# Six transformer layers with 16-head window attention: Wv times Wo formed per head on chip, values wide, no output projection

## The reference

```python
def shift_tokens(t):                       # second half of the channels comes from the token before
    a, s = jnp.split(t, 2, -1)
    s = jnp.pad(s, ((0, 0), (1, 0), (0, 0)))[:, :-1]
    return jnp.concatenate([a, s], -1)

def attn_layer(x, Wqkv, qs, ksc, Wo):      # 16 heads of 64: Wqkv 128 x 3072, Wo 1024 x 128
    q, k, v = sh(x @ Wqkv)
    q, k = l2norm(q) * qs, l2norm(k) * ksc
    q, k = rotary(q) * scale, rotary(k) / scale
    out = local_attention(q, k, v)         # window of 32 queries looks at its own 32 keys and the 32 before
    return out.transpose(0, 2, 1, 3).reshape(b, n, INNER) @ Wo
...
for i in range(DEPTH):                     # 6
    x = attn_layer(shift_tokens(x), Wqkv[i], q_scale[i], k_scale[i], Wo[i]) + x
    x = ffn_layer(shift_tokens(x), ln_g[i], ln_b[i], W1[i], b1[i], W2[i], b2[i]) + x
```

## Time and profile before

| | |
|---|---|
| median of 3 runs | 3265.14 us (3257.32 to 3265.72) |
| profiled execution, its own time | 3262.19 us |
| its span, first to last instruction | 3260.4 us |
| PE busy | 3129.7 us, 96% |
| ACT, DVE, POOL busy | 2717.7 (83%), 2687.9 (82%), 2560.2 (79%) |
| DMA, mean traffic | 69 GB/s; the one hardware queue takes 25.8% of the 16 engines' time |
| mean granted TensorE clock | 0.995 of full |

### The profile page before, as it was taken

How to read it: one execution, slowest core, us unless ns; L and a number is a source line. 1 busy time by engine, 2 the same in 40 slices (tenths; PEclk the granted TensorE clock), 3 DMA queues, 4 the chain that set the end, 5 groups by cost and what they waited for, 6 DMA issues and landing times.

```text
span 3260.4 us, 154019 instructions
## 1 busy us (share of the span) xinstructions
PE 3129.7 (96%) x65394; PEld 2384.6 (73%) x66148; DVE 2687.9 (82%) x4034; ACT 2717.7 (83%) x4817; POOL 2560.2 (79%) x2557
## 2 busy tenths in 40 slices
PE   8998799999999999999999999999999999999998
PEld 6886577777777777777777777777777777677776
DVE  6887888888888888888888888888888888788884
ACT  5665688888888888888888888888888888888886
POOL 3433988888888888888888888887888888788882
PEclk9999999999999999999999999999999999999999
DMA  1000332232233223223322322322332332332231
GB/s 47 29 2 28 83 79 73 75 78 68 71 75 86 69 71 80 70 64 88 82 61 74 79 67 77 85 70 63 78 78 72 78 75 67 86 75 62 65 76 52
DMA packets 140219, 224.69 MB, mean 69 GB/s; under 512 B 29456, under 2 KB 41360, under 8 KB 139152
## 3 DMA queue, kind: packets, MB, share of 16 engines
q1 hardware_dynamic: 139536, 214.78, 25.8%
HBM read 21.72 MB, written 4.19 MB: 8 GB/s over the span
## 4 chain that ended last, share of the span: by engine, by line
PE 93%; issue 3%; DVE 1%; POOL 1%; ACT 1%; DMA 0%; SPq 0%; POOLq 0%; DVEq 0%; ACTq 0%
PE bank L1021 12%; PE bank L954 11%; PE bank L906 11%; PE bank L1037 10%; PE bank L980 9%; PE bank L1367 8%; PE bank L907 7%; PE bank L999 5%; PE bank L1380 4%; PE bank L905 3%; PE bank L364 2%; PE bank L344 2%; PE bank L329 2%; PE bank L1352 1%; PE bank L1342 1%
## 5 line engine op out<-in xcount | busy, mean ns | idle before, releaser
L1284 POOL TENSOR_TENSOR rotbuf<-mbuf 128x512 f32<-128x512 f32 x768 | 975.1, 1275 | 340.4 <-PE bank L954 326.2
L1173 DVE TENSOR_TENSOR mbuf<-bank,table 128x512 f32<-128x512 f32 x768 | 522.5, 680 | 341.2 <-ACT sq L1063 290.0
L1298 POOL TENSOR_TENSOR rotbuf<-rotbuf,rs 128x512 f32<-128x512 f32 x768 | 788.9, 1043 | 14.9
L1063 ACT ACTIVATE sq<-bank 128x512 f32<-128x512 f32 x768 | 458.8, 597 | 154.7 <-PE bank L907 140.4
L1174 DVE TENSOR_TENSOR mbuf<-bank,table 128x512 f32<-128x512 f32 x768 | 522.8, 681 | 0.0
L906 PE MATMUL bank<-weights,inputs 128*128 128x512 bf16 x1152 | 438.4, 381 | 70.3 <-issue 45.3
L1021 PEld LDWEIGHTS bank<-probs_t,vbuf 64*64 64x64 f32 x24576 | 394.5, 134 | 115.7 <-issue 115.1
L954 PE MATMUL bank<-ident,rotbuf 128*128 128x128 f32 x3072 | 449.3, 279 | 17.6 <-POOL rotbuf L1298 7.8
L1155 DVE TENSOR_REDUCE ss<-sq 128x16 f32<-128x1024 f32 x384 | 459.4, 1196 | 0.0
L907 PE MATMUL bank<-weights,inputs 128*128 128x512 bf16 x1152 | 438.2, 380 | 0.0
L1021 PE MATMUL bank<-probs_t,vbuf 64*64 64x32 f32 x24576 | 437.3, 220 | 0.1
(11 more groups left out here) (119 smaller groups left out, 5736.5 us busy)
## 6 DMA issues: line engine op xcount, KB each, us to landing
vbuf<-v_stage SPq DMA_DIRECT2D x1152, 128.0 KB, 2.4
vbuf<-v_stage SPq DMA_DIRECT2D x576, 64.0 KB, 2.1
stage<-in_wqkv SPq DMA_DIRECT2D x36, 256.0 KB, 3.0
weights<-in_wo SPq DMA_DIRECT2D x6, 512.0 KB, 3.9
out_t<-weights SPq DMA_DIRECT2D x1, 2048.0 KB, 6.3
weights<-out_t SPq DMA_DIRECT2D x1, 2048.0 KB, 11.5
out_t<-weights SPq DMA_DIRECT2D x16, 128.0 KB, 2.0
wffn<-in_w SPq DMA_DIRECT2D x6, 341.0 KB, 3.1
```

The source lines that it names most:

```text
L1173: e.tensor_tensor(b.m1[:, u % 2, :].rearrange("p (h s d) -> p h s d", h=8, s=2), pj, cos, ALU.mult)
L1284: e.tensor_tensor(b.rot[:, u, :], b.m1[:, u % 2, :], b.m2[:, u % 2, :], ALU.add).then_inc(s.rotated, 1)
L1298: e.tensor_tensor(v, v, r, ALU.mult).then_inc(s.scaled, 1)
```

## The change

Out = sum over heads of P_h (x Wv_h) Wo_h is computed as sum over heads of P_h (x (Wv_h Wo_h)). Wv_h Wo_h is 128 x 128 for each head, formed once a layer on chip and split into bf16 hi and lo; the values of a token have 16 x 128 = 2048 columns (1024 before) in 8 parts; `pe_values_of` takes transposed probabilities as the stationary operand (4 heads x 32 keys on 128 partitions, 32 queries) and values as the moving one (128 columns), so that heads, key halves and head groups add up in one bank, tokens on partitions; two transposes (`pe_transpose_out`) take the place of `pe_project_out`. Keys, scores, masks and probabilities are kept in halves by even and odd window of 32. The freed bank becomes a fourth work bank. The weights carry Wv (transposed, with zeros for the other head of a pair) and Wo side by side in `wvo`; q and k columns come as `wqk`. Wo is no longer loaded on its own. All lists and the ring have a new order.

Core of the diff:

```diff
-PLACED = (160, 128)
+VALUE_COLS = HEADS * DIM
+VALUES = 2 * VALUE_COLS // 512
+PLACED = (256, 256)
...
+WORK_BANKS = 4
+FIRST_BANKS = 3
 WORK_RING = (
+    ("t", 3, 1), ("t", 4, 1), ("v", 0, 2), ("wv", 0, 1), ("out", 0, -1), ("pj", 3, 2), ("pj", 4, 2),
+    ("t", 5, 1), ("pj", 5, 2), ("v", 1, 2), ("up", 0, -2), ("up", 1, -2), ("t", 6, 1), ("pj", 6, 2),
+    ("v", 2, 2), ("pj", 7, 2), ("up", 2, -2), ("t", 7, 1), ("pj", 0, 3), ("v", 3, 2), ("v", 4, 2),
+    ("pj", 1, 3), ("mu", 0, -1), ("v", 5, 2), ("t", 0, 2), ("dn", 0, -2), ("t", 1, 2), ("pj", 2, 3),
+    ("v", 6, 2), ("v", 7, 2), ("t", 2, 2),
 )
...
-STAGE = 512
-STAGE_PIECES = 3 * INNER // STAGE
-STAGE_FROM, SPLIT_FROM, OUTER_AT = 2, 3, 4
-LATE_AT = {9: 0, 11: 1, 13: 2}
+STAGE, STAGE_FUSED = 512, 768
+SPLIT_PIECES, FUSED_PIECES = 2 * INNER // STAGE, VALUE_COLS // 512
+STAGE_PIECES = SPLIT_PIECES + FUSED_PIECES
+STAGE_FROM, SPLIT_FROM, FUSE_FROM, OUTER_AT = 3, 2, 5, 4
+LATE_AT = {11: 0, 13: 1}
...
+def fused_piece(k):
+    piece = k.seq - FUSE_FROM
+    return piece if k.ok and k.layer + 1 < DEPTH and 0 <= piece < FUSED_PIECES else None
...
-    col = 2 * INNER + 512 * half
+    col = 2 * INNER + 512 * part
...
-            e.wait_ge(s.att_ready, k.layer + 1)
...
+    staged = b.stage[:, (SPLIT_PIECES + i) % 2, :].rearrange("p (c r d) -> p c r d", c=2, r=3)
+    for group in range(4):
+        parity, chunk = divmod(group, 2)
+        mm = e.matmul(bank[:, DIM * group:DIM * (group + 1)], staged[:, chunk, parity, :], staged[:, chunk, 2, :], start=True, stop=True)
+    return mm
...
+def pe_fuse(e, s, b, at, ahead):
+    k = at(ahead)
+    i = fused_piece(k)
+    if i is None:
+        return
+    pe_wait_bank(e, s, at, "wv", 0)
+    e.wait_ge(s.staged[(SPLIT_PIECES + i) % 2], 16 * staged_count(k.layer + 1, SPLIT_PIECES + i))
+    fuse_products(e, b, work_bank(b, k, "wv", 0), i).then_inc(s.fused, 1)
...
+        return
+    e.wait_ge(s.fused, FUSED_PIECES * (k.layer + 1) + i + 1)
+    if i == 0 and k.layer > 0:
+        e.wait_ge(s.v_full, VALUES * (FIRST_N + k.layer * SEQS))
+    e.activation(b.wh[(k.layer + 1) % 2][:, fused_columns(i)], work_bank(b, k, "wv", 0)[:, :], ACT.Copy).then_inc(s.fused_hi, 1)
...
+    e.wait_ge(s.fused_hi, FUSED_PIECES * (k.layer + 1) + i + 1)
+    hi, lo = (w[(k.layer + 1) % 2][:, fused_columns(i)] for w in (b.wh, b.wl))
+    e.tensor_tensor(lo, work_bank(b, k, "wv", 0)[:, :], hi, ALU.subtract).then_inc(s.fused_lo, 1)
...
+    base = KEY_SLOT * (SLOTS * par + slot)
+    if window % 2:
+        first, step = base + 16 * (window - 1), KEY_ODD
+    else:
+        first, step = base + 16 * window, KEY_ODD - (WINDOW if window else 0)
+    return b.kflat[r, first:first + 2 * step].rearrange("p (a k) -> p a k", a=2)[:, :, 0:WINDOW]
-                              b.q[r, slot, first:first + WINDOW], b.k[r, k.par, slot, first:first + SPAN_K],
+                              b.q[r, slot, first:first + WINDOW], window_keys(b, r, k.par, slot, 4 * t + quarter),
...
-        e.wait_ge(s.out_copied, k.c[STEPS] + t)
-    for j in range(2):
-        for quarter in range(4):
-            for odd, parity in ((0, 0), (1, 1), (0, 1), (1, 0)):
-                r, out_r = slice(64 * odd, 64 * odd + 64), slice(64 * parity, 64 * parity + 64)
-                value = DIM_HEAD * (4 * half + 2 * j + parity)
-                prob = P * (2 * parity + j) + WINDOW * quarter
-                out = P * (2 * half + j) + WINDOW * quarter
-                mm = e.matmul(b.outs[odd][out_r, out:out + WINDOW], b.v[r, k.par, 4 * t + quarter, value:value + DIM_HEAD],
-                              b.deep_ptf[r, i % 2, prob:prob + WINDOW], start=True, stop=True)
+    terms = [(pair, odd, quarter) for pair in range(2) for odd in range(2) for quarter in range(4)
+             if 4 * t + quarter - (quarter % 2 != odd) >= 0]
+    for pair, odd, quarter in terms:
+        group = 2 * half + pair
+        block = 4 * t + quarter - (quarter % 2 != odd)
+        rows = slice(WINDOW * quarter, WINDOW * (quarter + 1))
+        prob = P * (2 * pair + odd) + WINDOW * quarter
+        mine = [x for x in terms if x[2] == quarter]
+        mm = e.matmul(b.out_nat[rows, DIM * t:DIM * (t + 1)], b.deep_ptf[:, i % 2, prob:prob + WINDOW],
+                      b.v[:, k.par, block, DIM * group:DIM * (group + 1)],
+                      start=half == 0 and (pair, odd, quarter) == mine[0], stop=half == 1 and (pair, odd, quarter) == mine[-1])
...
-def pe_project_out(e, s, b, at, ahead):
+def pe_transpose_out(e, s, b, at, ahead):
-    e.wait_ge(s.out_copied, k.c[STEPS] + STEPS)
-    out = work_bank(b, k, "out", 0)[:, 0:N_TOK]
-    for chunk in range(INNER // P):
-        mm = e.matmul(out, b.wo[k.layer % 2][:, chunk, :], b.ot8[:, chunk, :], start=chunk == 0, stop=chunk == INNER // P - 1)
-    mm.then_inc(s.proj_full, 1)
+    e.wait_ge(s.out_copied, k.c[1] + 1)
+    out = work_bank(b, k, "out", 0)
+    for t in range(2):
+        mm = e.transpose(out[:, P * t:P * (t + 1)], b.on[:, DIM * t:DIM * (t + 1)], b.ident[:, :])
+    mm.then_inc(s.out_full, 1)
...
-    t, half = divmod(i, 2)
-    e.wait_ge(s.v_full, k.c[4] + (i + 1))
-    if half == 0:
+    t, part = divmod(i, 4)
+    e.wait_ge(s.v_full, k.c[VALUES] + (i + 1))
+    if part == 0:
         e.wait_ge(s.v_placed[t], k.c[PLACED[t]])
...
+    if not k.ok:
+        return
+    e.wait_ge(s.pv_full, k.c[SUBS] + SUBS)
+    e.wait_ge(s.out_full, k.c[1])
+    e.activation(b.on, b.out_nat, ACT.Copy).then_inc(s.out_copied, 1)
...
-    e.tensor_tensor(b.probs[:, t, :, :].rearrange("p (b h) k -> p b h k", b=2), b.deep_scores,
-                    b.deep_max[:, t, :].rearrange("p (b h) -> p b h", b=2).unsqueeze(3).broadcast_to([P, 2, SLOTS, SPAN_K]),
-                    ALU.subtract).then_inc(s.shifted, 1)
+    e.tensor_tensor(b.probs[:, t, :, :, :].rearrange("p o h k -> p h o k"), b.scores_by_half,
+                    b.deep_max[:, t, :].unsqueeze(2).unsqueeze(3).broadcast_to([P, HEADS, 2, WINDOW]), ALU.subtract).then_inc(s.shifted, 1)
...
-    for odd in range(2):
-        r, col = 64 * odd, slice(512 * odd, 512 * (odd + 1))
-        e.wait_ge(s.v_copied, k.c[4] + (odd + 1))
-        e.dma_start(b.v[r + 32:r + 64, k.par, 0, :], b.vstage[0:32, 0, col]).then_inc(s.v_placed[0], 16)
-        e.dma_start(b.v[r:r + 64, k.par, 1, :], b.vstage[0:64, 0, col]).then_inc(s.v_placed[0], 16)
...
-        e.dma_start(b.v[r:r + 64, k.par, 7, :], b.vstage[64:128, 1, col]).then_inc(s.v_placed[1], 16)
+    for t in range(2):
+        for part in range(4):
+            e.wait_ge(s.v_copied, k.c[VALUES] + (4 * t + part + 1))
+            for block in range(4):
+                e.dma_start(b.v[WINDOW * part:WINDOW * (part + 1), k.par, 4 * t + block, :],
+                            b.vstage[WINDOW * block:WINDOW * (block + 1), t, 512 * part:512 * (part + 1)]).then_inc(s.v_placed[t], 16)
...
+def sp_stage_weights(e, s, b, layer, i):
+    taken = layer * STAGE_PIECES + i - 2
+    if taken >= 0:
+        of, piece = divmod(taken, STAGE_PIECES)
+        if piece < SPLIT_PIECES:
+            e.wait_ge(s.split, SPLIT_PIECES * of + piece + 1)
+        else:
+            e.wait_ge(s.fused, FUSED_PIECES * of + piece - SPLIT_PIECES + 1)
+    if i < SPLIT_PIECES:
+        e.dma_start(b.stage[:, i % 2, 0:STAGE], b.wqk[layer, :, STAGE * i:STAGE * (i + 1)]).then_inc(s.staged[i % 2], 16)
+    else:
+        e.dma_start(b.stage[:, i % 2, :], b.wvo[layer, :, i - SPLIT_PIECES, :]).then_inc(s.staged[i % 2], 16)
...
-        piece, rest = divmod(k.seq - STAGE_FROM, 2)
-        if rest == 0 and 0 <= piece < STAGE_PIECES:
-            sp_stage_attention(e, s, b, k.layer + 1, piece)
+        piece = k.seq - STAGE_FROM
+        if 0 <= piece < STAGE_PIECES:
+            sp_stage_weights(e, s, b, k.layer + 1, piece)
-    piece, rest = divmod(k.seq - SPLIT_FROM, 2)
-    if k.ok and k.layer + 1 < DEPTH and rest == 0 and 0 <= piece < STAGE_PIECES:
-        pool_split_attention(e, s, b, k.layer + 1, piece)
+    piece = k.seq - SPLIT_FROM
+    if k.ok and k.layer + 1 < DEPTH and 0 <= piece < SPLIT_PIECES:
+        pool_split_weights(e, s, b, k.layer + 1, piece)
```

More of the change, by code:

```diff
@@ L204, in first_bank @@
 def first_bank(b, kind, i):
-    return b.work[first_place(kind, i) % WORK_BANKS]
+    return b.work[first_place(kind, i) % FIRST_BANKS]
 def pe_first_wait_bank(e, s, at, kind, i):
     j, size = first_place(kind, i), len(FIRST_RING)
-    for back in range(WORK_BANKS, 6 * size, WORK_BANKS):
+    for back in range(FIRST_BANKS, 6 * size, FIRST_BANKS):
         slots = 0 if j >= back else 1 + (back - j - 1) // size
@@ L750, in __init__ @@
         self.x_ready, self.first_done = first.normed[1], FIRST_N + SEQS
-        self.att_staged = [sem(f"att_staged{i}") for i in range(2)]
-        self.att_hi = sem("att_hi")
-        self.att_split = sem("att_split")
+        self.staged = [sem(f"staged{i}") for i in range(2)]
+        self.split_hi = sem("split_hi")
+        self.split = sem("split")
+        self.fused = sem("fused")
```

(58 more changed lines are left out.)

309 lines of the change are left out of this document (158 added, 151 removed), and 4 rows, old and new, of the table WORK_RING.

## The result

The changed kernel takes 3772.95 us (median of four runs, 3771.47 to 3781.57), the kernel before 3261.23 on the same chip: 1.158 times as long, 95% interval 1.156 to 1.159. The forecast was 3898, the range 3630 to 4030. The profiled execution has a span of 3779.7, 519 more than before. Two single runs of later experiments, 5537 us in the one with merged transfers and 6053 us in the last, lie far above the other runs of the same kernel; the ratios leave them out.

The account below looks back on a forecast made before the run. PE bound the kernel before (93% of the span). Two waits on SP's transfers were to add 238 (76 slots) and 385 (20 slots), the start 10: +633 on 3260.4 = 3893, forecast 3898 us, range 3630 to 4030.

Parts of the forecast that it names:

- PE's own sum: PE's work in one slot: removed and added instructions sum to -1.39, a slot of 28.8 us if PE never waited.
- rival D: Values blocks: column groups of a 128-row tile take turns, +902 us on top, 4800 us; chance 4%.
- The first wait: Value placement: ACT's copy waits for 16 SP transfers, 13.7 us until PE may use the bank; normal slot 33.3 us.
- The second wait: PE's Wv-Wo product waits for a staged piece behind 32 placements, landing after 26.5 us; 20 slots of 49.4 us.
- The rest: At the start: four first pieces through PE, ACT, DVE and two more transfers add 10 us (5 to 20).
- The clock: PE after waits: falls to 1.2 GHz, 1.1 us a normal slot and 2.2 us a slot with a staged piece.
- Rival C: Both SP waits occur but the clock stays at 2.4 GHz: +502, 3767 us; chance 22%.
- the transport and lag terms: SP transfers: 0.72 us an issue, landings of 2.1 or 3.4 us; ACT's late serving adds 0.5 us a slot.
- Rival B: SP queue: the placement wait binds but a staged piece is never late: +328, 3593 us; chance 8%.
- Rival A: SP queue: neither wait is reached, needing an issue interval of 0.48 or less: -106, 3159 us; chance 4%.
- The zero for the fourth bank: PE's work banks: a fourth bank and the own order remove PE waits already about nil: 0.
- The other zero, for access patterns: Reordered halves of keys, probabilities and masks on DVE and ACT: 0, bounded by -0.2 and +1 us a slot.

Follow-up runs that it names:

- the last: Outer weights' 2 MB load issued as four 512 KB pieces in four successive slots, against the changed kernel with earlier staging and earlier placement: 3141.5 us, 0.964.
- the first experiment: SP stages each weight piece one slot earlier (STAGE_FROM 3 to 2), against the changed kernel: 3455.7 us, 1.060 of the kernel before.
- the version with both edits: Changed kernel with weight pieces staged one slot earlier and the first three blocks of a half placed as soon as free: 3150.4 us, 0.967.

## Why the prediction was right, and where its numbers were off

**PE's own sum** was right: 28.8 forecast, 28.55 with the waits gone. The four column groups of the 32-column tile work at once (1.89 a pair, as priced from two rows of other tiles), so rival D is out.

**The first wait** was right in place, count and size. Its terms: 13.5 for 13.7 and 18.2 for 18.04. What was too high is what I added: 0.5 for ACT's late copies (the measured loop has no such lag: a slot without a fall of the clock is 31.50, below even the 31.7), and 1.1 for the clock, as 1.4 us in three of four slots. It was 1.6 in 37 of 70, 0.85. Plain slots came to 32.35 for 33.3, which is some 65 us of the 125 by which the forecast was high.

**The second wait** was right: 24.8 us to the landing for 26.5, 47.6 for 49.4, another 35 us. The difference is the interval of the SP queue. I took 0.72 from a stretch of 18 placements, and that was a fair sample: over all 93 such stretches of the kernel before it is 0.717. In the changed kernel it is 0.69, and 21.28 / 32 = 0.665 in the slot shown. In both, most are 0.63 or 0.64 apart; what differs is how many hold SP for 1 to 2 us, 9% before and 7% after. Why was not tested.

**The rest:** six slots at the ends and with the 2 MB load stood in the sum at 3.1 us each and grew by some 5 together, and the fill grew by 6 for 10: some 18 us.

**The clock.** Rival C had both waits and a clock that stays up, and its time, 3767, is nearer to 3773 than mine. Its mechanism did not happen: the mean granted clock is 0.934 (0.995 before), the lower level stands in the windows above, and plain slots come in two lengths. The time agrees with C because the transport and lag terms, which C shares with the forecast, were about as much too high as the clock's price. A total that fits proves no mechanism; the slot lengths part by part do.

**Rival B** is what the first experiment made of the kernel: 3456 where I had 3593, for the same oversized plain slot (33.3, measured 32.15 there). **Rival A** (neither wait) is the version with both edits: 3150 where I had 3159. What I put against A was right: it would have needed an interval of 0.48 or less, and the interval is 0.69; that the two waits could be removed by moving when they start, not how long they take, the prediction did not ask.

**The zero for the fourth bank** held for the sum and was wrong as a reason. I argued that it removes waits that are already nil. It keeps nil a wait that the changed list has with three banks, 4.6 us a slot where nothing else holds PE; that the change's five more bank uses open it is argued. Had the diff kept three banks, the forecast would have had no term for it; what it would add beside the two waits was not run. The other zero, for access patterns, held: DVE, ACT and POOL work 25.3, 26.6 and 25.1 us in a full slot of 28.7, against 26.9 worked out for ACT.

**The rule weighed in the prediction** (the Trainium skill, "DMA: Bandwidth & Descriptors", "Rules for kernel authors": coalesce small transfers) is borne out in this case by the two runs on count and bytes: at the same bytes half the transfers (64 KB and not 32 KB each) took 444 us less. Followed to the letter it made this kernel slower, 3841 for 3773, because the merged transfers had to wait for data that is produced later.

## What to carry to other kernels

Count the transfers that a queue issues between the event that frees it and the first consumer, times its interval, and compare with the cover; bytes came second here, and a queue that waits half of the time can still set the pace when its work can only start at the end of a slot. When a change adds items ahead of an old one on an in-order queue, look at who takes the old one and how many slots lie between: one constant was worth 317 us. Look also at what the queue waits for ahead of an item: the wait, and not the 2 MB behind it, held SP in the slot of the outer weights. And count the uses of a ring of buffers a slot before and after a change; a buffer that costs and brings nothing today can be the one that a denser slot needs.
